# Second dense product of a mixture-of-experts stage, token-major: rows returned by way of HBM in place of result transposes

## The reference, cut to what matters

```python
x = x + _L0_conv_ref(_gn(x), ...)      # 3x3 convolution, 8 -> 8 channels, 256 x 256
x = x + _L1_conv_ref(_gn(x), ...)
x = x + _L2_conv_ref(_gn(x), ...)      # dense stage, below
x = x + _L3_conv_ref(_gn(x), ...)

# dense stage: B, E, N, D, F = 2, 8, 256, 256, 1024
h = jnp.einsum('bend,edf->benf', x, w1) + b1[None, :, None, :]
h = jax.nn.gelu(h, approximate=False)
out = jnp.einsum('benf,efd->bend', h, w2) + b2[None, :, None, :]
```

## Time and profile before

| | |
|---|---|
| median of 3 runs | 576.02 us (575.11 to 578.19) |
| profiled execution: its own time | 576.91 us |
| profiled execution: span of the records | 575.1 us |
| first two convolutions and their transposes | 0 to about 143 us |
| dense stage | about 143 to 499 us |
| last convolution | about 490 to 564 us |
| last stores land | 575.1 us |

### The profile page before, as it was taken

How to read it: one execution, slowest core, us unless ns; L and a number is a source line. 1 busy time by engine, 2 the same in 40 slices (tenths; PEclk the granted TensorE clock), 3 DMA queues, 4 the chain that set the end, 5 groups by cost and what they waited for, 6 DMA issues and landing times.

```text
span 575.1 us, 9042 instructions
## 1 busy us (share of the span) xinstructions
PE 520.0 (90%) x3326; PEld 255.5 (44%) x3326; DVE 374.1 (65%) x644; ACT 291.8 (51%) x354; POOL 159.1 (28%) x181
## 2 busy tenths in 40 slices
PE   0879999896979999999999999999999989978990
PEld 0534445364544444444444444444444545445440
DVE  4969999888766395194293392481547598678541
ACT  2599988333635453353362361461444828766510
POOL 4679888853270000000000000000000001677610
PEclk9889999898899999999999999999999999989996
DMA  8845555533020122022011112102123300134769
GB/s 327 324 111 146 150 132 139 143 101 147 0 75 1 73 74 74 0 73 73 0 73 73 31 42 73 73 0 73 74 74 108 112 0 2 45 81 107 242 200 349
DMA packets 14168, 57.41 MB, mean 100 GB/s; under 512 B 3116, under 2 KB 3244, under 8 KB 11052
## 3 DMA queue, kind: packets, MB, share of 16 engines
q1 hardware_dynamic: 11820, 49.30, 26.9%
q10 hardware_dynamic: 2316, 7.68, 3.7%
HBM read 30.03 MB, written 8.39 MB: 67 GB/s over the span
## 4 chain that ended last, share of the span: by engine, by line
PE 62%; DVE 19%; ACT 5%; POOL 4%; DMA 3%; issue 2%; ACTq 1%; SPq 1%; POOLq 0%; DVEq 0%
PE PS L1007 28%; PE PS L978 27%; DVE X L665 6%; DVE ST L626 6%; PE PS L878 2%; POOL XN L360 2%; ACT XN L439 2%; PE PS L952 2%; DMA X<-x 2%; PE PS L936 2%; PE PS L885 1%; DVE X L681 1%; ACT SCR L444 1%; DVE XT L674 1%; DVE SM L641 1%
## 5 line engine op out<-in xcount | busy, mean ns | idle before, releaser
L978 PE MATMUL PS<-XT,W1S 128*128 (+1 forms) x768 | 172.0, 383 | 1.7 <-DVE XT L674 1.7
L1007 PE MATMUL PS<-HID,W2S 128*128 128x512 f16 x768 | 170.8, 379 | 1.6 <-DVE W2S L688 1.6
L476 ACT ACTIVATE SCR<-PS,CONST 128x512 f32<-128x512 f32 x128 | 87.0, 686 | 64.4 <-PE PS L978 27.8
L978 PEld LDWEIGHTS PS<-XT,W1S 128*128 128x128 f16 x768 | 75.6, 99 | 91.1 <-issue 4.7
L1007 PEld LDWEIGHTS PS<-HID,W2S 128*128 128x128 f16 x768 | 75.1, 98 | 87.5 <-issue 1.8
L360 POOL TENSOR_TENSOR XN<-SCR,XN 128x1024 f16<-128x1024 f32 (+1 forms) x61 | 100.4, 1670 | 26.5 <-ACT SCR L444 26.5
L688 DVE SCALAR_TENSOR_TENSOR W2S<-W2F,W2S 128x2048 f16<-128x2048 f32 x10 | 22.9, 2291 | 114.6 <-ACT W2S L472 114.6
L333 POOL MEMSET HALO<- 48x520 f16 x12 | 6.3, 526 | 316.8 <-PE PS L978 316.3
L626 DVE BATCH_NORM_STATS2 ST<-X 128x6 f32<-128x512 f32 x128 | 81.5, 681 | 9.4 <-DMA X<-x 8.2
L439 ACT ACTIVATE XN<-X,SC 128x1024 f16<-128x1024 f32 (+1 forms) x61 | 64.1, 1050 | 33.9 <-POOL SC L351 27.6
L665 DVE SCALAR_TENSOR_TENSOR X<-PS,X 128x512 f32<-128x512 f32 x96 | 59.7, 680 | 21.5 <-PE PS L900 21.5
(11 more groups left out here) (47 smaller groups left out, 442.9 us busy)
## 6 DMA issues: line engine op xcount, KB each, us to landing
W1F<-w SPq DMA_DIRECT2D x10, 1024.0 KB, 4.7
W2F<-w SPq DMA_DIRECT2D x10, 1024.0 KB, 4.8
HALO<-XN SPq DMA_DIRECT2D x48, 129.9 KB
out<-X ACTq DMA_DIRECT2D x12, 512.0 KB, 6.8
HALO<-XN SPq DMA_DIRECT2D x48, 121.8 KB
X<-x SPq DMA_DIRECT2D x2, 2048.0 KB, 19.0
HALO<-XN SPq DMA_DIRECT2D x42, 64.9 KB
HALO<-XN SPq DMA_DIRECT2D x42, 60.9 KB
```

The costliest lines, as they stand in the source:

```text
L476: act.activation(SCR[:, ft % 2, 0:CH], bank(ft % G_RING), ACT.Gelu, bias=BT[:, ds(e * FT + ft, 1)], scale=1.0 / (XS * WS)).then_inc(gelu_o ...
L978: mm = pe.matmul(bank(ft % G_RING), W1S[:, w, h * NF + ft * P:h * NF + (ft + 1) * P], rhs, start=(n == 0), stop=(n == 3 * DH - 1))
L1007: mm = pe.matmul(bank(G2_BANK + h), W2S[:, w, ft * NW + h * P:ft * NW + (h + 1) * P], HID[slot][:, part, ft], start=(ft == 0 and part == 0 ...
```

## The change

The second product becomes token-major. The stationary operand is now a block of 128 tokens of `HID`, the moving operand the 256 output features of W2: 4 blocks to a pair, 24 matmuls of 256 columns each. ScalarE copies each block out of its bank (`copy_out`, 128x256, no bias), SyncE stores it to a buffer `yd` in HBM (512 B to a row) in the order of `X`, and the rows of a whole image come back by DMA into `YX`: first those of experts 0 to 6 (`load_first_experts`), then those of expert 7 (`load_last_expert`). VectorE adds them to `X` (`add_outputs`, both operands in SBUF). The bias is added to `X` by VectorE in the loop (`add_bias`). TensorE has no result transposes. Images 0 and 1 go through SyncE's queue behind the second pair of the end; image 3's first load is issued by ScalarE. In the last convolution the banks are a ring of 7, ScalarE issues the `halo_thirds` of step 8, and `store(1)` stands ahead of the last image's normalisation. GpSimd's order is nearly the same.

```diff
-L3_BANKS = (1, 2, 3, 0, 4)
+G2_BANK, TR_BANK, STAT_BANK, LAST_STAT_BANK = 4, 6, 5, 6
+L3_BANKS = (1, 2, 3, 0, 7, 4, 5)
...
-THIRDS_BY_ACT = ((0, 0), (11, 0), (11, 1),)
+THIRDS_BY_ACT = ((0, 0), (8, 0), (8, 1), (11, 0), (11, 1))
...
+    XT = at("XT", XY_OFF, [P, NB, DH, NE, 2, TOK], F16)
+    YT = at("YT", XY_OFF, [P, NB, NBLK, NE, NW], F32)
+    YX = at("YX", XY_OFF, [P, NB * IMG], F32)
...
+    YL = at("YL", XY_OFF + 2 * IMG * 4, [P, BLOCKS, NW], F32)
...
+    def y_last(p, k):
+
+        if p == 0:
+            return SCR[:, k // 2, CH + k % 2 * NW:CH + (k % 2 + 1) * NW]
+        return YL[:, k]
...
+    def load_outputs(queue, b, rows):
+        queue.dma_start(y_image(b)[rows].rearrange("p (k f) -> p k f", k=NBLK),
+                        yd[b][:, rows].rearrange("k p f -> p k f")).then_inc(y_in[b], 16)
+
+    def load_first_experts(queue, b):
+        for w in range(W2):
+            load_outputs(queue, b, slice(w * HALF_P, (w + 1) * HALF_P - R))
+
+    def load_last_expert(queue, b):
+        for w in range(W2):
+            load_outputs(queue, b, slice((w + 1) * HALF_P - R, (w + 1) * HALF_P))
...
+        def store_tokens(src, b, k, e, signal):
+
+            dst = yd[b, k].rearrange("(w c r) (t j) -> c (r t) w j", w=W2, c=NC, j=NJ)[e]
+            sp.dma_start(dst, src.rearrange("p (w j) -> p w j", w=W2)).then_inc(signal, 16)
+
+        def store_outputs(e, p, first):
+            for k in range(BLOCKS):
+                sp.wait_ge(yt_ok, first + k + 1)
+                store_tokens(y_tokens(e, p, k), 2 * p + k // NBLK, k % NBLK, e, y_out[p])
+
+        def store_last(n, k):
+            p = ENDING[n][1]
+            b = 2 * p + k // NBLK
+            sp.wait_ge(yt_ok, BLOCKS * (NPAIR * LAST + n) + k + 1)
+            store_tokens(y_last(p, k), b, k % NBLK, NE - 1, last_out[b])
...
-        for e in range(1, NE + 2):
+        for e in range(1, LAST + 1):
             load_w1(e)
             load_w2(e)
-        for g in range(8, 12):
+            for p in range(NPAIR):
+                store_outputs(e - 1, p, BLOCKS * (NPAIR * (e - 1) + p))
+
+
+        load_w1(LAST + 1)
+        load_w2(LAST + 1)
+        store_outputs(LAST, 0, BLOCKS * NPAIR * LAST)
+        load_w1(LAST + 2)
+        load_w2(LAST + 2)
+        sp.wait_ge(y_out[0], 16 * BLOCKS * (NE - 1))
+        sp.wait_ge(g1_mm, FT * (NPAIR * LAST + 2))
+        for b in range(2):
+            load_first_experts(sp, b)
+        for k in range(BLOCKS):
+            store_last(1, k)
+        for b in range(2):
+            sp.wait_ge(last_out[b], 16 * NBLK)
+            load_last_expert(sp, b)
+        load_w1(LAST + 3)
+        load_w2(LAST + 3)
+        store_outputs(LAST, 1, BLOCKS * (NPAIR * LAST + 2))
+        sp.wait_ge(x_new, X_NEW_AT["y", 0, NCH - 1])
+        sp.wait_ge(y_out[1], 16 * BLOCKS * (NE - 1))
+        load_first_experts(sp, 2)
+        load_ones(0)
+        store_last(3, 0)
+        store_last(3, 1)
+        sp.wait_ge(last_out[2], 16 * NBLK)
+        load_last_expert(sp, 2)
+        halo_half(8, 0)
+        store_last(3, 2)
+        store_last(3, 3)
+        halo_half(8, 1)
+        sp.wait_ge(last_out[3], 16 * NBLK)
+        load_last_expert(sp, 3)
+        for g in range(9, 12):
...
+        pool.wait_ge(g2_mm, BLOCKS * (2 * LAST + 3))
+        zero_pads(0, 1)
         pool.wait_ge(g1_mm, NE * NPAIR * FT)
         zero_halo(0, 1)
-        pool.wait_ge(g2_mm, 4 * (NE - 1) + 2)
-        zero_pads(0, 1)
         scale_and_bias(12)
         low_parts(8)
...
+        def copy_out(to, k, done):
+
+            act.wait_ge(g2_mm, done)
+            act.activation(to, bank(G2_BANK + k % 2)[:, 0:NW], ACT.Copy,
+                           scale=1.0 / (HS * WS)).then_inc(yt_ok, 1)
+
+        def out_block(e, p, k):
+            copy_out(y_tokens(e, p, k), k, e * (NPAIR * BLOCKS) + (p * BLOCKS + k + 1))
...
-        for k in range(len(ENDING) - 1):
-            ending_hidden(k)
-            for dh in range(DH):
-                ending_result(k, dh)
+        for n in range(3):
+            ending_hidden(n)
+            for k in range(BLOCKS):
+                ending_out(n, k)
...
+        act.wait_ge(y_out[1], 16 * BLOCKS * (NE - 1))
+        act.wait_ge(g1_mm, NE * NPAIR * FT)
+        load_first_experts(act, 3)
+        slot_free(8)
+        normalise_piece(FIRST_PIECE[8])
+        ending_out(3, 0)
+        normalise_piece(FIRST_PIECE[8] + 1)
+        ending_out(3, 1)
+        normalise_piece(FIRST_PIECE[8] + 2)
+        normalise_piece(FIRST_PIECE[8] + 3)
+        ending_out(3, 2)
+        thirds(8, 0)
+        normalise_piece(FIRST_PIECE[8] + 4)
+        ending_out(3, 3)
+        thirds(8, 1)
         for g in range(9, 11):
             normalise(g)
         store(0)
+        store(1)
         slot_free(11)
         for k in range(4):
             normalise_piece(FIRST_PIECE[11] + k)
-        last_thirds(0)
+        thirds(11, 0)
         normalise_piece(FIRST_PIECE[11] + 4)
-        last_thirds(1)
-        for b in range(1, NB - 1):
-            store(b)
+        thirds(11, 1)
+        store(2)
...
-        def mlp_chunk(b, i):
-            m = NCH * b + i
+        def add_outputs(b, i):
+
+            if i == 0:
+                dve.wait_ge(y_in[b], 16 * 2 * W2)
             xc = x_chunk(b, i)
-            dve.wait_ge(ty_mm, m + 1)
-            dve.tensor_tensor(xc, bank(TR_BANK + m % 2), xc, ALU.add).then_inc(x_new, 1)
+            dve.tensor_tensor(xc, y_chunk(b, i), xc, ALU.add).then_inc(x_new, 1)
+
+        def mlp_stats(b, i):
             dve.wait_ge(x_new, X_NEW_AT["y", b, i])
-            stats_chunk(12 + b, xc, i)
+            stats_chunk(12 + b, x_chunk(b, i), i)
+
+        def add_half(b, first):
+            for i in range(first, first + QUAD):
+                add_outputs(b, i)
+            for i in range(first, first + QUAD):
+                mlp_stats(b, i)
+
+        def add_bias(e):
+
+            for i in range(NCH):
+                xc = X[:, ds(e * IMG - (IMG - i * CH), CH)].rearrange("p (t j) -> p t j", j=NJ)
+                dve.tensor_tensor(xc, xc, B2.unsqueeze(1).broadcast_to([P, TC, NJ]), ALU.add
+                                  ).then_inc(bias_ok, 1)
...
+            add_bias(e)
...
         def in_third(ft):
-            if ft in (4, 7):
-                mlp_chunk(0, (4, 7).index(ft))
+            if ft == 4:
+                dve.wait_ge(bias_ok, NB * NCH)
+            if ft >= 4:
+                add_outputs(0, ft - 4)
 
         def in_fourth(ft):
+            if ft == 0:
+                deviation(12)
             if ft == 2:
-                mlp_chunk(1, 2)
                 variance(12)
-            if ft in (4, 6):
-                mlp_chunk(1, ft // 2 + 1)
-
-        w2_parts(LAST)
-        ending_hidden(0)
-        w2_parts(LAST + 1)
-        ending_hidden(1)
+            if ft >= 2:
+                add_outputs(1, ft - 2)
+
+        for n in range(2):
+            w2_parts(LAST + n)
+            ending_hidden(n)
+            next_w1(LAST + n + 1)
         w2_parts(LAST + 2)
         ending_hidden(2, in_third)
-        for i in range(2, NCH):
-            mlp_chunk(0, i)
+        next_w1(LAST + 3)
+        for i in range(QUAD):
+            mlp_stats(0, i)
+        add_half(0, QUAD)
         aggregate(12)
-        mlp_chunk(1, 0)
-        mlp_chunk(1, 1)
-        deviation(12)
         w2_parts(LAST + 3)
         ending_hidden(3, in_fourth)
-        for i in range(5, NCH):
-            mlp_chunk(1, i)
+        for i in range(6, NCH):
+            add_outputs(1, i)
+        for i in range(NCH):
+            mlp_stats(1, i)
         aggregate(13)
         deviation(13)
+        add_outputs(2, 0)
+        add_outputs(2, 1)
...
+            tokens = slice(k * P, (k + 1) * P)
+            to = bank(G2_BANK + k % 2)
             for ft in range(FT):
-                if h == 0:
+                if k == 0:
                     pe.wait_ge(hid_ok, ready + (ft + 1))
-                if ft == 0 and h == 0:
+                if ft == 0 and k == 0:
                     pe.wait_ge(w2_ok, load + 1)
-                for part, w in ((0, 0), (1, 0), (0, 1)):
-                    mm = pe.matmul(bank(G2_BANK + h),
-                                   W2S[:, w, ft * NW + h * P:ft * NW + (h + 1) * P],
-                                   HID[slot][:, part, ft],
-                                   start=(ft == 0 and part == 0 and w == 0),
+                for part, w in PRODUCTS:
+                    mm = pe.matmul(to[:, 0:NW], HID[slot][:, part, ft, tokens],
+                                   W2S[:, w, ft * NW:(ft + 1) * NW],
+                                   start=(ft == 0 and part == w),
                                    stop=(ft == FT - 1 and w == 1))
+                if ft == FT - 1:
+                    mm.then_inc(g2_mm, 1)
                 if between is not None:
-                    if ft == FT - 1:
-                        mm.then_inc(g2_mm, 1)
-                    between(ft)
-            if between is None:
```

(18 more changed lines are left out.)

319 lines of the change are left out of this document (128 added, 191 removed).

## The result

The changed kernel takes **594.69 us** (median of 4 runs, 591.66 to 595.19), the kernel before beside it 577.11 us (575.11 to 578.24): a ratio of 1.030 (95% interval 1.025 to 1.035). The forecast was 571.3 us, with a range that ended at 579. It was wrong in sign. The profiled execution spans 593.4 us, against 575.1.

What follows compares the result with a forecast made beforehand. TensorE was taken as the bound, 62% of the span and always busy in the expert loop. Terms: -1.9 us up to image 0, +2.1 thirds, +1.9 to image 3, -6.8 tail, total -4.7: 571.3 us, range 566 to 579.

Steps and rivals of the forecast that it cites:

- Costed at nothing: Items priced at zero across the kernel: bias adds, copies, SyncE's stores, the returning rows, VectorE's adds, shorter writes of XT.
- Image 0's rows: Third pair of the end: images 0 and 1 return 3.7 MB in 9.9 us at 370 GB/s, 3 us to spare.
- out and in, 4.7 us at most each: Expert 7's rows, stored and loaded back from 447.5 on, are there at 457 at the latest.
- rows that return late: Rival, chance 0.10: VectorE waits for image 0 in the third pair, stopping three engines; 8 us late gives 579.3 us.
- The stores ahead of image 3: Last convolution: ScalarE issues eight stores first, four more at 1.1 us each; image 3 at +2.1 instead of -0.6.
- The tail's gain: After the last update: image 1's stores have long gone, taking 6.8 us off the 11.1 of stores alone.
- The last image: From image 3's normalisation start to the last update: 26.7 us, kept unchanged, last update at 566.1.
- From image 1 to image 2: Last convolution, between the two normalisation starts: no change, 15.4 us as before.
- gaps: Tiles that come late: 0.7 us idle for expert 0's first half and two pairs of the end, +2.1 in all.
- the third pair: End of the dense stage: 22.2 us instead of 27.6, with result transposes and waits for VectorE gone, -5.4.
- the halo thirds on ScalarE: Last convolution: four transfers ahead of image 0's last piece, 2.76 us less 0.7 for shorter copies, +2.1.
- The fourth pair: End of the dense stage: its hidden -0.2, from there to ScalarE's start of image 0's normalisation -0.3.

Runs made afterwards that it cites:

- no_return: Changed kernel with no rows loaded back; the adds read the image's own chunk twice, so the second product's sum is missing: 578.8 us, ratio 1.0035.
- store1_late: Changed kernel with image 1's stores back behind the last piece of image 3's normalisation on ScalarE: 594.3 us.
- one_load_t8: Changed kernel with one late 128-partition return load per image, W1F before the last stores, image 1's stores and step 8's thirds on SyncE: 578.8 us, 1.0045.
- mix_sp: Changed kernel: one load for images 0 and 1, whole-then-short for 2 and 3; image 1's stores, step 8's thirds on SyncE; image 3's second adds earlier: 576.9 us, 1.0003.
- whole_loads: Changed kernel with each image's first return load as one transfer of 128 partitions instead of two halves of 56: 585.0 us, ratio 1.014.
- before_store1: Kernel before with image 1's stores put ahead of image 3's pieces on ScalarE: 576.6 us, ratio 0.9987.

## Why the prediction was wrong

**The step that failed** stands under "Costed at nothing": "Image 0's rows ... 9.9 us at the 370 GB/s of the start ... 3 us to spare". The 370 GB/s is the rate of loads over 128 partitions, and was applied to loads over 56 and 8, in whose windows 191 to 197 and 114 to 132 GB/s were moved. The first rows took some 20 us instead of 9.9. The second step that fails follows from it: "out and in, 4.7 us at most each". Out took 12.55 us behind the first loads, so the last expert's rows were asked for only at 461.75, and they came at 468.4, 11 us after the forecast's 457. The rival "rows that return late" was the right one, with 0.10: "it costs its lateness, and once more as SyncE has the next W1 load behind it". VectorE waited 9.22 us, and the pair took 33.9 us instead of 22.2, 11.7 more. The lateness counted once; W1F behind it added the 1.17 us wait for a copy, and TensorE's granted clock after its idle time was 0.67 from 462 to 470 us and 0.75 from 470 to 480. Without a return it took 22.0 and the whole was 15.9 us faster, with full width alone 9.7.

**Not in the sum at all** was image 2. Its rows return by the same slow loads, VectorE waits 8.56 us for them ahead of image 1's variance, and image 0 to 1 takes 21.3 us instead of 19.1. With whole loads it is 18.9. In after TensorE waits 8.10 us in this step for the halo rows of image 0, until 520.52.

**The stores ahead of image 3** (+1.9 forecast, against image 2): the issue was counted, at 1.1 us each, the wait of the last store for image 1's last update was not. In the kernel before that is +5.2 us, and the halo rows beside the stores add 0.7. In after no store waited, and the issue was the mis-sized term: 1.7 us each for six, a little over the prediction's upper bound of 1.6. The tail's gain was right: -7.0 in after, -5.6 alone, -6.8 forecast.

**The last image** (kept at 26.7): 29.4 us. TensorE's waits of after from 500 us on (us in total, times, longest), then the windows to the last update of before and of after:

```profile
PE PS L1013 <- DMA HALO<-XN: 19.3, 2, 11.2
```

```profile
537.00:564.00 27.00, 24.95 (x290) 11.35 (x288) 12.39 (x20) 9.96 (x10) 8.57 (x7) 1.00 0.72 221
```

```profile
560.00:589.00 29.00, 21.51 (x228) 9.47 (x228) 9.60 (x16) 9.91 (x10) 8.35 (x5) 0.82 0.75 246
```

The longer of the two waits ends at 565.87, 5.9 us into the last image's stretch: TensorE stands still for the halo rows of image 2, whose issues cost SyncE 1.46 us each on the mean (0.60 to 2.46 in the chain) while ScalarE issues its stores. The clock granted after it is 0.82 on the mean, part of it at the lower of its two levels (0.42 us a matmul for 0.21). Before, it is 1.00, and TensorE never waits for halo rows there.

**From image 1 to image 2** (kept at 15.4) it takes 16.6 to 16.7 us in every row of the table with loaded rows. The rows of after have the collision in it: GpSimd's four low parts take 7.49 us there instead of 6.49, and its last one 2.35 instead of 2.05, together 1.3. In `no_return`, where VectorE pays instead (7.09 us for four adds at 513.32), the step is 15.6. No run tests it apart.

**What held.** An output at 10.48 us (10.5 forecast, +1.5 us in 14); gaps of 0.56 and 0.52 us in two pairs of the end, a little under 0.7; the third pair once its rows are there, 22.0 to 22.4 against 22.2; the halo thirds on ScalarE, 1.9 against 2.1. The fourth pair was to gain 0.5 us; with the rows in time it lost 0.3 to 0.6, in after 2.1, where VectorE's late work for image 0 stands ahead of its mean. The bias adds and the copies did stay hidden: the loop's outputs follow one another without idle.

The parts of the loss sum up: +2.0 to the third pair, +6.3, +2.1, +4.3, +1.2, +6.7, +2.7, and -7.0 in the tail, the 18.3 us of span. The experiments attribute 15.9 of it to the return (medians). The stores' place explains 5.4 of the 6.7 (21.2 against 15.8 in `store1_late`) and most of the -7.0, for nothing on balance. That `one_load_t8` with 22.2 us in the third pair still ended 0.45% above before shows that the 5.4 us gained there are eaten by the last stage. In its trace image 0 to 1 takes 21.2 us, although its thirds are on SyncE, which is image 2's late rows (2 us of the whole by `mix_sp`), and the last image 33.7, which is the wait for halo rows and the clock that follows; the last two were seen, not tested apart. What would undo them stays open.

## What to carry to other kernels

Price a transfer by the rate of a row with the same number of partitions, and read share and rate of a window together: here a busy share of 0.93 at half the rate was a narrow transfer, not a lack of requests. A store in the same queue pays for it too: 12.55 us instead of 1.8. In a queue, what an edit costs is the wait of the instruction that is moved, semaphore and all, and then everything behind it; two of my steps, one in the prediction and one in an experiment, counted only the issue. Rows that go out and come back have a last piece that nothing can start early, so look at when that piece is asked for, not at the sum of the bytes.

## What the runs showed of the hardware

- A load into the 56 partitions of one half moved 191 to 197 GB/s at a DMA share of 0.90 to 0.93, one into 128 moved 410 at 0.98, and two halves issued at once by two engines 220 at 0.91.
- VectorE with two inputs in SBUF and GpSimd with its low parts held each other up: 8.08 us for four adds instead of 2.48 in whole_loads, or, with the adds unhindered, 4.47 us for one low part instead of 2.07 in after. The Trainium skill states an exclusive lock between the two for this case ("SBUF — State Buffer", section "SBUF: two separate sides"). The trace agrees.
- Moves of 256 columns with a load of 98 ns each, all on 128 rows, run at 109 ns a piece (10.48 us / 96), so the loads are fully hidden. The rule of the Trainium skill that the prediction weighed ("TensorE: Matmul & The Clock Gate", Part 3, The mechanism) did not hold here.
- The issue of a halo transfer cost SyncE 0.64 us in a quiet stretch, and 0.6 to 2.5 us, 1.46 on the mean, while ScalarE issued stores (after and before_store1).
- Small stores of 128 KB landed 1.8 us after their issue (median of 56), and four issued behind the narrow loads 15.2 us after it.
